# Projecting attention's convolved chunks in pairs over two PSUM banks

## The reference, cut to what matters

```python
proj = einsum('bld,pd->blp', hidden_states, in_proj_w)        # gate, hbc, dt
hbc  = proj[..., I:I + CONV_DIM]                              # B, C and x of the group
conv = conv_bias; for k in range(4): conv += pad[:, k:k+L, :] * conv_weight[:, k]
xBC  = silu(conv)                                             # six chunks of 128 channels
state = state * dA_t + dtx_t * B_t ; y_t = state @ C_t        # done as masked matrix products
y    = (y + x * D); yn = rmsnorm(y) * norm_weight * silu(gate)
out  = yn @ out_proj_w.T
# FFN: weights are looked up by 8 bit planes: a tree of selections over a table of 256 values
```

## Time and profile before

| what | value |
|---|---|
| median of three runs | 3618.82 us |
| the profiled execution's own time | 3620.42 us |
| its span, from first to last instruction | 3618.7 us |
| mean granted clock of TensorE | 0.99 |
| TensorE busy | 3519.7 us, 97% |
| VectorE busy | 3082.9 us, 85% |
| ScalarE busy | 1459.2 us, 40% |
| GpSimd busy | 468.5 us, 13% |

### The profile page before, as it was taken

How to read it: one execution, slowest core, us unless ns; L and a number is a source line. 1 busy time by engine, 2 the same in 40 slices (tenths; PEclk the granted TensorE clock), 3 DMA queues, 4 the chain that set the end, 5 groups by cost and what they waited for, 6 DMA issues and landing times. The chain is left out here.

```text
span 3618.7 us, 58730 instructions
## 1 busy us (share of the span) xinstructions
PE 3519.7 (97%) x19789; PEld 2875.8 (79%) x19789; DVE 3082.9 (85%) x4879; ACT 1459.2 (40%) x2218; POOL 468.5 (13%) x298
## 2 busy tenths in 40 slices
PE   6699999999999999999999999999999999997999
PEld 4488888888888888888888888888888888886888
DVE  6599999999999999999999999999999999997343
ACT  3444444444444344444344444444444434442111
POOL 3100111100111100111110011110011111001333
PEclk9799999999999999999999999999999999998999
DMA  7623244323533343324433353334332452334331
GB/s 247 244 99 128 102 163 164 116 110 128 191 111 128 125 175 135 123 98 167 168 111 116 128 186 116 128 118 176 141 114 106 164 172 110 116 127 119 103 92 56
DMA packets 220672, 490.29 MB, mean 135 GB/s; under 512 B 39594, under 2 KB 85066, under 8 KB 211042
## 3 DMA queue, kind: packets, MB, share of 16 engines
q1 hardware_dynamic: 216388, 488.86, 38.5%
q0 software_dynamic: 304, 0.82, 0.1%
q10 hardware_dynamic: 3952, 0.27, 0.1%
HBM read 320.51 MB, written 169.39 MB: 135 GB/s over the span
## 5 line engine op out<-in xcount | busy, mean ns | idle before, releaser
L790 PE MATMUL bank<-ht,wt 128*128 128x512 f32 x7680 | 1862.4, 397 | 8.0 <-DMA ht<-h_d 8.0
L790 PEld LDWEIGHTS bank<-ht,wt 128*128 128x128 f32 x7680 | 1425.6, 188 | 354.4 <-issue 19.2
L1012 DVE SCALAR_TENSOR_TENSOR xc<-bank,cvw,xc 128x496 f32<-128x496 f32 (+2 forms) x1152 | 820.7, 717 | 96.7 <-ACT xc L927 45.8
L927 ACT ACTIVATE xc<-bank,cvb,cvw 128x512 f32<-128x512 f32 x384 | 299.7, 781 | 1128.1 <-PE bank L790 1128.1
L885 PE MATMUL bank<-wot,gy 128*128 128x512 f32 x3072 | 738.2, 396 | 0.0
L885 PEld LDWEIGHTS bank<-wot,gy 128*128 128x128 f32 x3072 | 567.3, 188 | 128.3 <-issue 11.0
L766 POOL TENSOR_TENSOR r<-rv,neg_half 128x4 f32<-128x4 f32 x64 | 90.5, 1413 | 2490.7 <-DVE rv L1100 2490.7
L1034 DVE TENSOR_TENSOR m<-cbm,y 128x1024 f32<-128x1024 f32 x256 | 301.5, 1219 | 7.8
L763 POOL TENSOR_TENSOR segr<-adts,mask_le 128x1024 fp32r<-128x1024 f32 x128 | 242.8, 1919 | 377.9 <-DVE adts L1003 377.9
L917 ACT ACTIVATE gy<-z 128x512 fp32r<-128x512 f32 x256 | 162.1, 633 | 320.5 <-DVE z L1074 320.5
L913 ACT ACTIVATE z<-bank 128x512 f32<-128x512 f32 x256 | 150.5, 588 | 278.7 <-PE bank L790 278.7
(11 more groups left out here) (166 smaller groups left out, 3048.0 us busy)
## 6 DMA issues: line engine op xcount, KB each, us to landing
ht<-h_d SPq DMA_DIRECT2D x64, 2048.0 KB, 7.9
acc<-acc_d SPq DMA_DIRECT2D x64, 1024.0 KB, 7.2
wt_d<-wnext SPq DMA_DIRECT2D x128, 512.0 KB, 3.1
acc_d<-acc SPq DMA_DIRECT2D x64, 1024.0 KB, 4.3
wt<-wt_d SPq DMA_DIRECT2D x70, 512.0 KB, 8.4
stage<-in_L_attn_in_proj_w SPq DMA_DIRECT2D x106, 256.0 KB, 2.8
h_d<-ht_out SPq DMA_DIRECT2D x8, 2048.0 KB, 8.2
wot<-wt_d SPq DMA_DIRECT2D x28, 512.0 KB, 6.3
```

The costliest lines, as they stand in the source:

```text
L790: ins = pe.matmul(pb[:, :], wt[:, n, l, k, :], ht[:, rr, k, :], start=(q == 0 and k == 0), stop=(q == 2 and k == KC - 1))
L927: act.activation(xc[:, n, :], bank[PROJ_BANK[n]][:, :], ACT.Identity, bias=cvb[:, n:n + 1], scale=cvw[:, n, TAPS - 1:TAPS]).then_inc(s_tap, 1)
L1012: ins = dve.scalar_tensor_tensor(dst, src, cvw[:, n, TAPS - 1 - k:TAPS - k], dst, ALU.mult, ALU.add)
```

## The change

Chunks 0 to 5 are projected as the pairs (0, 1), (2, 3) and (4, 5). Within a pair the matmuls alternate: for each pass and slice first the one chunk's matmul and then the other's, with the same moving tile `ht` and the chunk's own weights, each into its own bank. A pair's two chunks are so complete one matmul apart. Banks are dealt anew: chunks 2 and 3 go to banks 6 and 7, which hold the scans, the products and the squares later, chunk 4 to bank 2, chunks 5, 8 and 9 to bank 0, chunk 6 to 1, chunk 7 to 2. TensorE's waits move with the banks. On VectorE the first two leaves of the tree go ahead of the convolutions, the other two behind the second convolution, `find_here` stays behind the last.

```diff
-PROJ_BANK = (0, 1, 2, 0, 1, 2, 0, 1, 2, 0)
+PROJ_BANK = (0, 1, 6, 7, 2, 0, 1, 2, 0, 0)
...
-                        def project(n):
-                            pe.wait_ge(s_wt[n], 16 * g + 16)
-                            pb = bank[PROJ_BANK[n]]
+                        def project(*chunks):
+                            for n in chunks:
+                                pe.wait_ge(s_wt[n], 16 * g + 16)
                             for q, (l, rr) in enumerate(PASSES):
                                 for k in range(KC):
-                                    ins = pe.matmul(pb[:, :], wt[:, n, l, k, :], ht[:, rr, k, :],
-                                                    start=(q == 0 and k == 0), stop=(q == 2 and k == KC - 1))
-                            ins.then_inc(s_proj, 1)
+                                    for n in chunks:
+                                        ins = pe.matmul(bank[PROJ_BANK[n]][:, :], wt[:, n, l, k, :], ht[:, rr, k, :],
+                                                        start=(q == 0 and k == 0), stop=(q == 2 and k == KC - 1))
+                                        if q == 2 and k == KC - 1:
+                                            ins.then_inc(s_proj, 1)
...
-                        for n in range(NCV):
-                            if n == 0:
-                                pe.wait_ge(s_z, CT * it + CT)
-                            elif n == 2:
-                                pe.wait_ge(s_acc, TT * it + 1)
-                            elif n >= 3:
-                                pe.wait_ge(s_conv, NCV * it + n - 2)
-                            project(n)
+                        pe.wait_ge(s_z, CT * it + CT)
+                        project(0, 1)
+                        pe.wait_ge(s_rv, it + 1)
+                        pe.wait_ge(s_y, CT * it + CT)
+                        project(2, 3)
+                        pe.wait_ge(s_acc, TT * it + 1)
+                        pe.wait_ge(s_conv, NCV * it + 1)
+                        project(4, 5)
 
                         pe.wait_ge(s_segr, 2 * it + 4)
                         pe.wait_ge(s_acc, TT * it + TT)
-                        pe.wait_ge(s_y, CT * it + CT)
                         for q in range(SEGB):
+                            if q == 1:
+                                pe.wait_ge(s_conv, NCV * it + 4)
...
-                        pe.wait_ge(s_conv, NCV * it + 4)
                         project(NCV)
 
                         pe.wait_ge(s_silu, NCV * it + 2)
-                        pe.wait_ge(s_rv, it + 1)
...
                             else:
-                                pe.wait_ge(s_z, CT * it + CT + 2)
+                                pe.wait_ge(s_z, CT * it + CT + 1)
...
-                        pe.wait_ge(s_z, CT * it + CT + 1)
+                        pe.wait_ge(s_z, CT * it + CT + 3)
                         project(NCV + 3)
...
-                        pe.wait_ge(s_z, CT * it + CT + 3)
                         pe.wait_ge(s_nlo, 2 * it + 2)
...
+                            pair(0, la, 0)
+                            pair(1, lb, 0)
                             for n in range(NCV):
...
-                                if n == 2:
-                                    pair(0, la, 0)
-                                elif n == 3:
-                                    pair(1, lb, 0)
-                                elif n == 4:
+                                if n == 1:
                                     pair(2, lc, 0)
-                                elif n == 5:
                                     pair(3, ld, 0)
+                                elif n == NCV - 1:
                                     find_here(0)
```

## The result

The changed kernel takes 3692.9 us (median of four runs, 3690.57 to 3693.82) against 3618.9 before: the ratio is 1.0203, with a 95% interval from 1.0185 to 1.022. The forecast was 3619, and its range ended at 3640. The profiled execution has a span of 3692.1 us, 73.4 more than before.

What follows compares the result with a forecast made beforehand. Attention was taken as bound by TensorE's string of matmuls end to end. Spacing 0 plus waits 0 on the median of 3618.82 gave 3619 us; its own range was 3612 to 3626, the 8-in-10 range 3556 to 3640.

Steps and rivals of the forecast that it cites:

- The spacing: Paired projections, 4608 matmuls changing bank each time: taken as 0, bounded between 62 us less and 5 us more.
- half and whole gain: Bank changes bring paired projections closer: half 31 us less, 3588, chance 0.16; whole 62 us less, 3557, chance 0.14.
- The clock: TensorE's clock in the pairs: expected at 1.00; rival has it fall, 891 us more, 4510, chance 0.02.
- The step that failed: VectorE: leaves 0 and 1, 0.54 us each, fit inside the 0.8 us wait for tap 0, so cost nothing.
- The idle time for the 1.1 us of two free leaves: VectorE before the convolutions: must wait 0.8 us for tap 0; without it the leaves would cost up to 1.1.
- one of the signs that the prediction named as showing it wrong: Listed signs: pair spacing of 220 to 227, TensorE waiting for dtx or conv, clock under 1.00 inside attention.
- TensorE's other waits: Waits moved among the 120 projections and in the first scan: all covered, sum-of-squares wait unchanged, 0 in all.
- the stretch behind: VectorE from convolution 4 to dtx 3: cbm 0.65 us later, dtx 3 about 0.4 late, covered by a tenth.
- The rival on the slower side: VectorE 3% late from convolution 4 to dtx 3, holding TensorE in the first scan: 19 us, 3638, chance 0.10.
- The range's upper end: Whole kernel: 3640, top of the range holding 8 in 10, 3556 to 3640, which takes in VectorE late.

Runs made afterwards that it cites:

- the three runs: Kernel before with projections ordered slice by slice, output matmul passes reordered, or output passes outermost with a bank change every matmul: 3618.55, 3618.4 and 3619.65 us.
- the second experiment: Changed kernel, leaves still ahead of the convolutions, with GpSimd's segr made to wait until all four leaves are done: 3619.83 us, ratio 1.0005.
- the first experiment: Changed kernel with leaves 0 and 1 moved from ahead of the convolutions to behind the second one, beside leaves 2 and 3: 3618.88 us, ratio 0.9999.
- the kernel with the leaves alone: Kernel before, without pairs and with its old banks, only leaves 0 and 1 moved ahead of the convolutions: 3820.64 us in one run.

## Why the prediction was wrong, step by step

**The spacing** was taken as 0 out of bounds from 62 us less to 5 more, and that was right: 233.4 ns in pairs. The likeliest case was chosen for the right reason, the equal rows across a change of bank. The chances of half and whole gain, 0.30 together, rested on an unexplained 4.5 ns of the output matmuls, which the pairs and the three runs show not to come from a change of bank or from repeated tiles. The clock was taken as 1.00 through the pairs, and that was right too (1.00 in the row of 50.22 us above); they leave TensorE no idle time, so no run tells what alternating banks with idle time between would do.

**The step that failed** is the one on VectorE: "Leaves 0 and 1 (0.54 each) go ahead of the convolutions", inside idle time, and "nothing moves on GpSimd's queue". The second half is true and was the trap. Because `adts` stays ahead of the leaves, GpSimd starts its two `segr` at the moment when VectorE starts the leaves. They measured 2.05 and 2.13 instead of 0.54 each, 3.1 us more. In the attention of the kernel before no leaf stood beside a `segr`, only convolutions did, and I took the price of a leaf by itself. But the trace of that kernel had the price, in its first stage, which none of my rows shows. There GpSimd copies `xp` (line 271) while VectorE works through leaves of the same operation, shape and type (line 507). One copy, the leaf beside it, and the next leaf, which has no copy beside it:

```profile
71.07 3.87 POOL L271 COPY xp<-xb 128x2048 f32<-128x2048 f32 x1 [7.99 <-DMA xb<-in_x]
```

```profile
71.71 3.53 DVE L507 TENSOR_SCALAR leaf<-mask,lut 128x512 int32<-128x512 int32 x1
...
76.37 0.53 DVE L507 TENSOR_SCALAR leaf<-mask,lut 128x512 int32<-128x512 int32 x1
```

The copy ends at 74.94 and the leaf at 75.24, again some 0.3 behind. Four of this stage's 32 leaves stand beside a copy, and all four are held up so: they last 1.88 to 3.95 us and end 0.28 to 0.29 behind it, while the other 28 take 0.53 to 0.55. From these the forecast could have taken the bound: if a leaf cannot run beside a `segr`, both end with the second one, 2 x 1.92 behind `adts`.

The idle time for the 1.1 us of two free leaves was itself read rightly: the second experiment still waits 0.76 for the tap with both leaves done, and the prediction's times leave 0.8 (1013.19 - 1012.4).

**What the traces show of the two engines:** a leaf that starts 0.15 us after a `segr` ends 0.28 after it ends, and the second `segr`, which starts while leaf 0 runs out, is held up by 0.18: the two last 3.97 together, against 3.79 in the second experiment, where no leaf is beside them. Convolutions beside `segr` are not touched, 4.36 with it and 4.36 without in that same experiment. The Trainium skill ("SBUF — State Buffer", the section "Who interferes with whom") has a rule for this: VectorE and GpSimd share one pair of ports, which is locked for a whole instruction, so that the second to come is blocked; `tensor_scalar` can run in a mode that takes the pair, and an instruction outside such modes with at most one operand read from SBUF does not. The trace agrees with it in all three, 2.05 and 2.13 for the leaves, 0.18 for `segr` and 4.36 for the convolutions. The runs show that the two exclude each other, not through which port.

**From 3.1 to 1.0.** The chain goes: leaf 1 ends at 8.77 us after the iteration's start; the first convolution starts at 8.69 instead of the first experiment's 6.45 (1010.54 - 1004.09; the forecast had the tap done at 6.34), 2.24 late. Convolution 2 no longer waits for its tap (0.25 in the second experiment), and convolution 3 ends near 18.2 (1140.85 + 4.36 - 1126.99) instead of 16.35, 1.9 late. The forecast had it 0.9 early for the second half of the segment sums, so it is now 1.0 late, which is what the row shows. So of 3.1 us on VectorE two thirds fell into slack, and with one leaf's 1.5 all of it did. This is one of the signs that the prediction named as showing it wrong, TensorE waiting "for conv before the segment sums"; the wait stands between their two halves.

**TensorE's other waits** came as forecast: none in the first scan, none at chunks 2 to 8, and 45.7 us before the sum of squares. The taps run at 5.64, forecast near 5.6. Where the leaves are out of `segr`'s way, the stretch behind is right too: in the first experiment `cbm` stands at 1026.32 - 1004.09 = 22.23, forecast 22.25, and dtx 3 ends 0.35 after the scan row starts (forecast 0.6), without a wait.

**The rival on the slower side** had the right engine and the wrong place: VectorE late by 3% everywhere and felt at the scan, for 19 us. It was late by 3.1 us in one place and felt at the segment sums. The range's upper end came from that rival, so it fell with it.

## What to carry to other kernels

Before an instruction is moved into an engine's idle time, look at what the other engines do in that time, above all GpSimd beside VectorE: a duration read where an instruction ran alone is no price for it there. Another stage of the same trace may hold the two side by side, as the first stage did here. A release that starts two engines at the same moment makes them neighbours in every iteration. And a loss behind a slack has a threshold: one held-up leaf cost nothing here, two cost 74 us.

## What was not expected of the hardware

- An int32 leaf of 0.54 us on VectorE takes 2.05 to 2.13 when it starts just behind a `segr` of 1.92 on GpSimd, and 0.54 again when the `segr` is moved away. In the first stage the same leaf takes up to 3.95 beside a copy of 3.88.
- In the kernel with the leaves alone, TensorE's clock was granted at 0.50 for 3.4 us in each of 20 iterations after a wait of some 2.5 us. Why only in every third or fourth iteration is open. A wait of 1.0 us in every iteration of the changed kernel left the clock at 1.00.
- Matmuls of 128x128 by 128x512 stay 233 ns apart in projections and 229 in output matmuls, whatever the order of banks, weights and moving tiles was made to be. The cause stays open.
